# First layer of a gated cross-attention pair: the next batch's second key projection one step later, and two reorderings at the start of a batch

## What is computed

```python
x = x + tanh(g_xattn[0]) * attention(layernorm(x), ctx)     # 16 heads of 64, causal: q0.., k0.., v0..
n = layernorm(x)
h = rmsnorm(n)                                               # gamma1
q, k, v = h @ Wq + bq, ...((h @ Wdown + bdown) @ Wup + bup)
att = softmax(einsum('bthd,btgd->bthg', q, k) / sqrt(16))    # per token, head against head
out = einsum('bthg,btgd->bthd', att, v)                      # the "per-token output", o
y = n + (out @ Wo + bo)                                      # moe_residual
x = x + tanh(g_ffn[0]) * (y + sum_e gate_e * rmsnorm(y) @ We)
```

## Time and profile before

| | us |
|---|---|
| median of 3 runs (lowest, highest) | 2502.51 (2501.88, 2504.15) |
| the profiled execution | 2502.84 |
| its span in the trace | 2501.0 |

### The profile page before, as it was taken

One profiled execution on the slowest core, in us unless ns is written; L12 is line 12 of the kernel. 1 busy time (PEld: TensorE's weight loads), 2 busy tenths in 40 slices (PEclk: granted clock), 3 DMA queues, 4 the chain that ended last, 5 costly groups with the idle time before them and its releaser, 6 DMA issues.

```text
span 2501.0 us, 47888 instructions
## 1 busy us (share of the span) xinstructions
PE 2227.4 (89%) x16000; PEld 1887.5 (75%) x16000; DVE 1480.4 (59%) x3922; ACT 1267.7 (51%) x3969; POOL 1023.1 (41%) x907
## 2 busy tenths in 40 slices
PE   5888899898888888888875799999999999999998
PEld 4667677777777777777664688888888888888888
DVE  4466666767667676676767635555555555555551
ACT  5655655556555565555633434455544444445541
POOL 1255555565555655556446213333332322333320
PEclk9999999999999999999977799999999999999999
DMA  4000000000000000000110200000000000000000
GB/s 154 8 12 14 6 17 17 17 13 4 17 17 17 13 4 17 17 17 4 39 32 13 110 16 7 13 17 17 17 17 17 17 17 16 5 13 17 17 9 9
DMA packets 26000, 51.40 MB, mean 21 GB/s; under 512 B 6160, under 2 KB 7312, under 8 KB 24784
## 3 DMA queue, kind: packets, MB, share of 16 engines
q1 hardware_dynamic: 25936, 50.57, 6.0%
HBM read 42.17 MB, written 8.39 MB: 20 GB/s over the span
## 4 chain that ended last, share of the span: by engine, by line
PE 57%; DVE 15%; ACT 8%; POOL 6%; issue 6%; DVEq 4%; POOLq 2%; DMA 0%; ACTq 0%
PE l_ffn L1714 13%; POOL l_prod L385 5%; PE l_ffn L161 4%; PE l_attn L161 4%; PE l_ffn L162 4%; PE l_ffn L163 4%; PE l_attn L1675 4%; PE l_attn L163 3%; PE l_attn L162 3%; DVEq L735 3%; PE l_side L161 3%; PE l_heads L1689 2%; POOLq L355 2%; PE l_side L163 2%; PE l_side L162 2%
## 5 line engine op out<-in xcount | busy, mean ns | idle before, releaser
L1253 POOL TENSOR_SCALAR l_probs<-l_probs,l_rinv 128x256 f32<-128x256 f32 x512 | 240.3, 484 | 479.2 <-DVE l_rinv L1492 478.3
L1376 ACT ACTIVATE l_probs<-l_score,l_negmax 128x256 f32<-128x256 f32 x512 | 239.1, 474 | 268.2 <-DVE l_negmax L1487 268.1
L385 POOL TENSOR_TENSOR l_prod<-l_att,l_kv 128x2048 f32<-128x2048 f32 x64 | 288.5, 4542 | 164.6 <-DVE l_att L672 164.6
L371 POOL TENSOR_TENSOR l_prod<-l_q,l_kv 128x2048 f32<-128x2048 f32 x64 | 291.2, 4561 | 150.7 <-DVE l_att L655 86.6
L1714 PE MATMUL l_ffn<-l_w,l_hid 128*128 128x256 f32 x1536 | 348.6, 381 | 1.0 <-ACT l_hid L1337 1.0
L1714 PEld LDWEIGHTS l_ffn<-l_w,l_hid 128*128 128x128 f32 x1536 | 286.2, 190 | 48.8 <-issue 12.7
L1499 DVE COPY l_probsT<-l_attn 128x512 f32<-128x512 f32 x240 | 164.5, 686 | 142.8 <-PE l_attn L1675 142.8
L745 DVE CUSTOM_DVE_ANT_0 l_probs<-l_score,l_mbias 128x256 f32<-128x256 f32 (+1 forms) x512 | 161.3, 352 | 144.9 <-PE l_score L947 95.8
L678 DVE TENSOR_REDUCE l_h<-l_prod 128x128 f32<-128x2048 f32 x64 | 146.3, 2286 | 107.5 <-POOL l_prod L385 107.2
L468 ACT ACTIVATE l_probs<-l_probs,l_negmax 128x256 f32<-128x256 f32 x256 | 130.8, 511 | 107.7 <-DVE l_negmax L745 106.6
L1487 DVE TENSOR_REDUCE l_negmax<-l_score 128x2 f32<-128x512 f32 x256 | 175.0, 684 | 15.0 <-PE l_score L1663 13.7
(11 more groups left out here) (261 smaller groups left out, 7177.2 us busy)
## 6 DMA issues: line engine op xcount, KB each, us to landing
l_ctxin<-in_ctx SPq DMA_DIRECT2D x32, 256.0 KB, 3.0
l_xin<-in_x SPq DMA_DIRECT2D x16, 256.0 KB, 2.6
l_x<-in_x SPq DMA_DIRECT2D x16, 256.0 KB, 2.6
x<-l_acc SPq DMA_DIRECT2D x16, 256.0 KB, 2.0
l_xin<-x SPq DMA_DIRECT2D x16, 256.0 KB, 3.1
l_x<-x SPq DMA_DIRECT2D x16, 256.0 KB, 2.6
out<-l_x SPq DMA_DIRECT2D x16, 256.0 KB, 2.0
l_hid<-in_w SPq DMA_DIRECT2D x2, 1536.0 KB, 8.2
```

What stands on the lines that cost most here:

```text
L371: nc.gpsimd.tensor_tensor(prod[:, u].rearrange("p (h g d) -> p h g d", h=half, g=H), q4[:, u * half:(u + 1) * half].unsqueeze(2).to_broadc ...
L385: nc.gpsimd.tensor_tensor(prod[:, u].rearrange("p (h d g) -> p h d g", h=half, d=HD), a4.unsqueeze(2).to_broadcast([P, half, HD, H]), v4.u ...
L1253: last = nc.gpsimd.tensor_scalar(probs[:, j % 4, t * S:(t + 1) * S], probs[:, j % 4, t * S:(t + 1) * S], rinv[:, j, t:t + 1], 1.0, ALU.mul ...
L1376: last = nc.scalar.activation(probs[:, s % 4, t * S:(t + 1) * S], ps[:, t * S:(t + 1) * S], ACT.Exp, bias=negmax[:, s, t:t + 1], accum_out ...
```

## The change

Three edits, all in the first layer. The next batch's second key projection k1 goes from step 11 to step 12 in `ahead_at`; with the table it moves in TensorE's and ScalarE's programs and in `attn_uses`, where it now stands between T9 and T10. At the start of a batch, TensorE projects q0 and q1 ahead of the transposes of o, and ScalarE copies them ahead of the high half. VectorE takes the variance of x1 ahead of the low half.

```diff
@@ -211,7 +211,7 @@
 
 
     own_at = {0: "k3", 1: "v1", 2: "v3", 3: "q2", 5: "q3"}
-    ahead_at = {9: "k0", 10: "xT", 11: "k1", 13: "v0", 16: "k2", 19: "v2"}
+    ahead_at = {9: "k0", 10: "xT", 12: "k1", 13: "v0", 16: "k2", 19: "v2"}
     attn_uses = ["q0", "q1"]
     for s in range(STEPS):
         attn_uses += [f"T{s - LAG_T}"] * (LAG_T <= s < H + LAG_T)
@@ -535,11 +535,11 @@
 
         def body(a, b, c, nxt):
             yield BEGIN
-            if c is not None:
-                high(side, "oT", c, foT[0], foT_hi)
             if a is not None:
                 project("q0", a)
                 project("q1", a)
+            if c is not None:
+                high(side, "oT", c, foT[0], foT_hi)
             for s in range(STEPS):
                 yield s - 0.6
                 if s >= 1:
@@ -821,11 +821,11 @@
 
         def body(a, b, c, nxt):
             yield BEGIN
-            if c is not None:
-                low(side, "oT", c, foT, foT_hi)
             if b is not None:
                 dve.drain()
                 variance(x1, statB, mvB, varB, varB_ready)
+            if c is not None:
+                low(side, "oT", c, foT, foT_hi)
             yield BEGIN_OUT
             if c is not None:
                 moe_residual(c)
@@ -1020,13 +1020,13 @@
 
         def body(a, b, c, nxt):
             yield BEGIN
-            if c is not None:
-                pe.wait_ge(gathered, 4 * (c + 1))
-                transpose4(side, "oT", c, o)
             if a is not None:
                 attn.emptied(pe, "xT", a)
                 project("q0", a)
                 project("q1", a)
+            if c is not None:
+                pe.wait_ge(gathered, 4 * (c + 1))
+                transpose4(side, "oT", c, o)
             yield BEGIN_OUT
             if c is not None:
                 side.emptied(pe, "oT", c)
```

## The result

The changed kernel takes 2525.87 us, median of four runs (2523.78 to 2531.17), against 2502.20 us for the kernel before; the ratio is 1.0099, with a 95% interval from 1.0080 to 1.0117. It is **slower by 1%, 23.7 us**; spread over the 14 batches that would be 1.7 us each. (The ratio is an estimate over all the runs, not the quotient of the two medians, which is 1.0095.) The profiled execution's span is 2525.2 us.

A forecast was written before the change was run, and what follows sets the result against it. Both ends bound a batch: GpSimd's path ends it, with TensorE 1.5 us ahead. Per batch, 2.1 less 2.5 plus 1.2 plus 0.1 is 0.9 us; times 14, 13 us on 2502.5 gives 2516 us, range 2494 to 2530.

The forecast's parts named there:

- The bound and its move: End of a batch: GpSimd's path, last before, gets 2.3 us shorter and is no longer last; TensorE is.
- v0's wait: TensorE before v0: stands still some 5.7 us for ScalarE's copy of k1, behind the exponential; v0 starts 2.1 us later.
- Waits absorbed: TensorE from v0 to the output projection: a late TensorE meets fewer waits, 2.5 us saved (2.2 to 2.8).
- The clock behind v0: TensorE's v0 after its standstill: half clock costs 1.2 us per batch, between nothing and 2.3 us.
- Rival (c): Behind v0: half clock begins only as v0 does, lasts 3.4 to 5 us, costs 1.7 to 2.3 per batch; 18%.
- The start of a batch: Projection's end to the residual addition: the gather wait goes, a wait for the halves replaces it; 0.1 us more.
- The variance: VectorE, ahead of the low half: costs and gives nothing, covered by TensorE's 2.9 us of q0 and q1.

The follow-up runs named there:

- the wait filled: All three edits, plus 40 extra matmuls of 128x256 in TensorE's wait before v0: 2506.59 us, ratio 1.0020 to the kernel before.
- The delay of 0.47 us: The kernel before, plus 4 extra matmuls of 128x256 between the transposes and q0 at the start of each batch: 2518.41 us, ratio 1.0073.

## Why the forecast was right, and where its sizes were off

- **The bound and its move.** Right. TensorE's late v0 took the end of the batch from GpSimd, whose path was to be 2.3 us shorter. It starts 2.5 us earlier by the rows and ends 1.35 earlier; VectorE's L757 still waits 1.10 us for TensorE (at 729.44), so TensorE is the last.
- **v0's wait.** Right in cause, place and size: 5.7 us forecast, 5.25 measured, put down to L460, and down to 1.5 us when the copy goes first. v0 was to start 2.1 us later; it did by 1.85 (10.09 less 8.24).
- **Waits absorbed.** 2.5 forecast. Before, from v0 to the end of the projection are 24.8 us (687.42 to 712.22); with the wait filled 22.0 to L757, which starts 0.03 behind the projection's end. So 2.8 us, the upper end given.
- **The clock behind v0: the first term that was mis-sized.** 1.2 forecast, 2.4 measured, just over the upper end of 2.3. The forecast took the slow stretch behind k1, 3.4 us, as the nearest row and let part of it lie inside the wait. Part of it did, 1.1 to 4.2 us. What failed is the length: the clock was low for 6.8 us in the batch at 705.37 and 10.2 us in that at 867.71, so that 4.5 to 6.2 us of it were left behind v0's start in the 13 batches. Half of that, 2.2 to 3.1 us, is near what was paid. The rule of the Trainium skill named in the forecast ("TensorE: Matmul & The Clock Gate", "HAM oscillation — how this bites in real kernels") has such a loop pay in every turn, and the trace agrees: half clock behind every one of the 14 waits of 4.2 to 5.3 us. Rival (c) was right on the price, not on the cause it gave: the half clock did not begin only as v0 does.
- **The start of a batch.** 0.1 forecast; 6.44 us before, and 6.42 after (729.40 to 735.82), from the end of the projection to L685. Right, but only against the kernel before: against the old start under the same conditions it costs 1.7 us (4.68 and 6.39), which the forecast's sum hid, as the old start would have lost its wait too.
- **The variance.** Forecast at nothing while q0 and q1 cover it. By itself its order costs 0.25 us per batch, 3.5 in all, and the kernel lost 19, most of it by the clock. In all edits together its share wasn't taken apart.
- **What was missing.** 1.85 less 2.8 plus 2.4 is 1.45 us per batch against the clean batches of before (78.4); the mean after is 80.7, 2.3 more. The rest is the slow first halves, 39.81 against 38.9, 0.9. Against the mean of before (78.7), which has slow stretches of its own, the loss is 2.0. The forecast took the first half as untouched, since no instruction in it moved. The delay of 0.47 us shows that this is wrong here. That the total came within 10 us of the forecast is partly luck: the batches of the trace lost 2.0 us each where 0.9 was forecast, and 4.4 us came back in a part of the program that no edit touches.

## What to carry to other kernels

When a producer is moved in a shared ring of banks, go through what its copy-out queues behind on the copying engine at the new place; here one copy behind an exponential that waits for a third engine made 5.25 us of standstill and half clock in it and after it, and the same move with the copy ahead of it won 1.1%. An edit that frees one wait should be costed against the old order under the new conditions, not against the old trace alone. And where TensorE's clock falls once per turn of a loop, a change of a few tenths of a microsecond can cost or save several times its length, so a loss that small edits seem to cause has to be tested with a plain delay.

## What the runs showed of the hardware

- The granted clock fell to half inside waits of TensorE of 5.25 us, 1.1 to 4.2 us before the next matmul, and stayed low for 4.5 to 6.2 us behind its start. This cost 2.4 us per batch, and 40 matmuls of 128x256 put into the wait took it away in all 13 batches.
- It fell to half in the first half of a batch without a long wait ahead: 0.40 and 0.27 us of waiting and 12 matmuls of 8 columns stood before it. In identical work it came in some batches and not in others (4 of 13 before, 12 of 13 with the wait filled), starting some 17 to 19 us behind L685.
- One slow stretch there of 3.4 us costs 1.5 us of the batch (38.9 to 40.4), one twice as long 3.1 (42.0).
- 8 matmuls of 128x256 in waits that were there anyway left no such stretch in the traces of two kernels (0 of 13), and 2, 4 and 7 of 13 in those of three others. Why not all there isn't settled; the rows show that the clock fell and after what, not by which measure.
